# Query halves turned by DMA in an attention and FFN kernel: raw fp16 halves, inverse norms multiplied into the scores

## What is computed

```python
q = (x @ Wq.T).reshape(b, s, H, HD).transpose(0, 2, 1, 3)
k = (x @ Wk.T).reshape(b, s, HKV, HD).transpose(0, 2, 1, 3)
q = _rmsnorm(q, q_norm_w)      # tf * rsqrt(mean(tf * tf) + EPS) * w
k = _rmsnorm(k, k_norm_w)
qg = q.reshape(b, HKV, G, s, HD)
scores = jnp.einsum('bkgqd,bksd->bkgqs', qg, k) / math.sqrt(HD)
attn = jax.nn.softmax(scores + bias[None], axis=-1)
...
return out @ Wo.T
```

## Time and profile before

| what | value |
|---|---|
| median of 3 runs | 728.1 us (727.3 to 729.38) |
| the profiled execution's own time | 728.39 us |
| its span, first to last instruction | 725.1 us |
| PE busy | 709.9 us, 98% |
| DVE, ACT, POOL busy | 497.4, 453.3, 452.4 us |
| share of the chain that ended last on PE | 86% |
| DMA, share of 16 engines | 21.7% |

### The profile page before, as it was taken

One profiled execution on the slowest core, in us unless ns is written; L12 is line 12 of the kernel. 1 busy time (PEld: TensorE's weight loads), 2 busy tenths in 40 slices (PEclk: granted clock), 3 DMA queues, 4 the chain that ended last, 5 costly groups with the idle time before them and its releaser, 6 DMA issues.

```text
span 725.1 us, 14838 instructions
## 1 busy us (share of the span) xinstructions
PE 709.9 (98%) x5322; PEld 429.3 (59%) x5322; DVE 497.4 (69%) x777; ACT 453.3 (63%) x1325; POOL 452.4 (62%) x380
## 2 busy tenths in 40 slices
PE   9999999999999999999999999999989999999996
PEld 8766565665656566565665656566535555555554
DVE  5978777577666757767675775575665777777776
ACT  0578475764856667484574747547556677767664
POOL 0468774844855675484376648438427778868885
PEclk9999999999999999999999999999999999999999
DMA  7410433242332232234233122221000000010001
GB/s 263 180 61 2 171 107 106 83 133 72 116 131 91 98 124 64 72 116 159 72 116 130 58 78 82 74 74 30 2 1 1 0 1 0 1 44 17 0 1 58
DMA packets 21737, 54.18 MB, mean 75 GB/s; under 512 B 3744, under 2 KB 4288, under 8 KB 19520
## 3 DMA queue, kind: packets, MB, share of 16 engines
q1 hardware_dynamic: 21552, 53.41, 21.7%
q10 hardware_dynamic: 144, 0.26, 0.1%
HBM read 51.57 MB, written 2.10 MB: 74 GB/s over the span
## 4 chain that ended last, share of the span: by engine, by line
PE 86%; POOL 5%; DVE 4%; DMA 2%; issue 1%; SPq 1%; ACT 1%; DVEq 0%; POOLq 0%
PE bank L561 20%; PE bank L563 20%; PE bank L562 20%; PE bank L698 3%; PE bank L901 3%; PE bank L902 3%; PE bank L876 3%; PE bank L877 3%; PE bank L740 2%; POOL wqlo L1883 1%; DMA xT<-in_xt 1%; PE bank L888 1%; PE bank L705 1%; PE bank L889 1%; PE bank L725 1%
## 5 line engine op out<-in xcount | busy, mean ns | idle before, releaser
L561 PE MATMUL bank<-wohi,oThi 128*128 128x512 f16 x256 | 97.1, 379 | 2.1 <-DVE oTlo L1577 2.1
L561 PE MATMUL bank<-wqhi,cThi 128*128 128x512 f16 x256 | 97.0, 379 | 1.4 <-POOL wqlo L1883 0.6
L563 PE MATMUL bank<-wohi,oTlo 128*128 128x512 f16 x256 | 97.0, 379 | 0.0
L562 PE MATMUL bank<-wolo,oThi 128*128 128x512 f16 x256 | 97.0, 379 | 0.0
L563 PE MATMUL bank<-wqhi,cTlo 128*128 128x512 f16 x256 | 97.0, 379 | 0.0
L562 PE MATMUL bank<-wqlo,cThi 128*128 128x512 f16 x256 | 97.0, 379 | 0.0
L1900 POOL TENSOR_TENSOR qinv<-qms,neghalf 128x8 f32<-128x8 f32 x32 | 52.7, 1646 | 46.5 <-ACT qms L1074 46.5
L1893 POOL TENSOR_TENSOR wolo<-wor,wohi 128x512 f16<-128x512 f32 x32 | 36.4, 1157 | 70.8 <-ACT wohi L1037 70.8
L1066 ACT ACTIVATE qsq<-qraw 128x128 f32<-128x128 f32 x256 | 75.8, 299 | 4.7
L1585 DVE SCALAR_TENSOR_TENSOR x<-bank,ysc,x 128x512 f32<-128x512 f32 x64 | 48.0, 750 | 44.2 <-PE bank L563 43.7
L1907 POOL TENSOR_TENSOR qn<-qraw,qinv 128x512 f32<-128x512 f32 x64 | 68.6, 1092 | 4.2 <-POOL qinv L1900 3.2
(11 more groups left out here) (209 smaller groups left out, 1886.0 us busy)
## 6 DMA issues: line engine op xcount, KB each, us to landing
wqr<-in_wq SPq DMA_DIRECT2D x8, 1024.0 KB, 4.8
wor<-in_wo SPq DMA_DIRECT2D x8, 1024.0 KB, 4.8
raw<-in_gu_w SPq DMA_DIRECT2D x28, 256.0 KB, 2.9
zeros<-in_gu_z SPq DMA_DIRECT2D x28, 256.0 KB, 3.6
wkvr<-in_wkv SPq DMA_DIRECT2D x8, 512.0 KB, 4.2
srow<-in_up_s SPq DMA_DIRECT2D x14, 256.0 KB, 4.2
raw<-in_dn_w SPq DMA_DIRECT2D x14, 256.0 KB, 3.2
zeros<-in_dn_z SPq DMA_DIRECT2D x14, 256.0 KB, 4.5
```

The source lines that it names most:

```text
L561: mm(o, ahi, bhi, start=start and k == 0, stop=False)
L562: mm(o, ahi, blo, start=False, stop=False)
L563: last = mm(o, alo, bhi, start=False, stop=stop and k == n - 1)
```

## The change

The inverse norm no longer touches the queries. POOL scales the raw query tile by a power of two and rounds it to fp16 (`query_high`, the new high half), DVE computes the low half from the same raw tile (`queries_low`), and both go side by side into `qpair`, rows on partitions. Four DMA transposes for two tiles, eight a unit, turn `qpair` into `qT`, each for one batch slot of 32 rows: 32 partitions x 16 blocks x 128 values of 2 bytes, 128 KB (`turn_queries`). Sixteen small DMAs a unit (32 partitions x 4 floats) carry the inverse norms from the row layout of the queries to the row layout of the scores (`move_norms`). DVE multiplies them by the constant factor (`qsc`), multiplies the scores by `qsc`, and then adds the bias in an instruction of its own. `transpose_q` and `queries_high` are gone.

```
+TURNED = 16 * 2 * BQ
+MOVED = 16 * BQ
...
-        qn = sb("qn", [P, HQ, G, HD], F32, att)
+        qpair = sb("qpair", [P, HQ, 2, G, HD], F16, att)
...
-        qhi = sb("qhi", [P, HB, G, S], F16, att)
-        qlo = sb("qlo", [P, HB, G, S], F16, att)
+        qT = sb("qT", [P, 2, BQ, 2, 2, G, S], F16, att)
...
+            def turn_queries(u, j):
+                if u and j == 0:
+                    sp.wait_ge(t_s, u)
+                sp.wait_ge(d_qlo, HQ * u + 2 * j + 2)
+                for b in range(BQ):
+                    sp.dma_start(qT[:, j, b, :, :, :, :].rearrange("p t k g s -> p (t k g) s"),
+                                 qpair[S * b:S * b + S, 2 * j:2 * j + 2, :, :, :].rearrange("p t k g d -> p (t k g) d"),
+                                 transpose=True).then_inc(l_qT, 16)
+
+            def move_norms(u):
+                sp.wait_ge(p_qpow, 2 * u + 2)
+                if u:
+                    sp.wait_ge(d_qsc, u)
+                for b in range(BQ):
+                    for g in range(G):
+                        sp.dma_start(qmoved[S * g:S * g + S, b, :], qinv[S * b:S * b + S, g, :]).then_inc(l_qsc, 16)
...
                 load_up(first)
                 load_down(first)
+                turn_queries(2 * kv, 0)
+                turn_queries(2 * kv, 1)
+                move_norms(2 * kv)
                 load_gate(second)
                 load_up(second)
                 if kv + 1 < HKV:
                     load_wo(kv + 1)
                 load_down(second)
+                turn_queries(2 * kv + 1, 0)
+                turn_queries(2 * kv + 1, 1)
+                move_norms(2 * kv + 1)
...
             def scores(u):
                 pe.wait_ge(d_klo, u + 1)
-                pe.wait_ge(d_qlo, HQ * u + HQ)
+                pe.wait_ge(l_qT, TURNED * u + TURNED)
+                if not (isinstance(u, int) and u == 0):
+                    pe.wait_ge(d_sc, u)
...
-                    if not (isinstance(u, int) and u == 1 and t == 0):
-                        for tq in queries_after(t):
-                            transpose_q(u, tq)
...
             def queries_low(u, t):
-                dve.wait_ge(a_qhi, HQ * u + t + 1)
-                V.tensor_tensor(qlo[:, BQ * t:BQ * t + BQ, :, :].rearrange("p b g s -> p g b s"),
-                                query_bank(u, t)[:, :].rearrange("p (g b s) -> p g b s", g=G, b=BQ),
-                                qhi[:, BQ * t:BQ * t + BQ, :, :].rearrange("p b g s -> p g b s"),
-                                ALU.subtract).then_inc(d_qlo, 1)
+                dve.wait_ge(p_qhi, HQ * u + t + 1)
+                V.scalar_tensor_tensor(qpair[:, t, 1, :, :], qraw[:, t, :, :], V_DOWN, qpair[:, t, 0, :, :],
+                                       ALU.mult, ALU.subtract).then_inc(d_qlo, 1)
 
             def scores_biased(u, kv):
                 first = isinstance(u, int) and u == 0
+                dve.wait_ge(l_qsc, MOVED * G * u + MOVED * G)
+                V.tensor_scalar(qsc[:, :, :], qmoved[:, :, :].rearrange("p b t -> p t b"), scale[:, 0:1], None,
+                                ALU.mult).then_inc(d_qsc, 1)
                 dve.wait_ge(t_s, u + 1)
...
-                V.scalar_tensor_tensor(sc[:, :, :], PB[1][:, :].rearrange("p (b k) -> p b k", k=S), scale[:, 0:1],
-                                       bias[:, None, :].broadcast_to([P, HB, S]), ALU.mult,
-                                       ALU.add).then_inc(d_sc, 1)
+                V.tensor_tensor(sc[:, :, :], PB[1][:, :].rearrange("p (b k) -> p b k", k=S),
+                                qsc[:, :, :].rearrange("p t b -> p (t b)")[:, :, None].broadcast_to([P, HB, S]),
+                                ALU.mult).then_inc(d_scaled, 1)
+                dve.wait_ge(d_scaled, u + 1)
+                V.tensor_tensor(sc[:, :, :], sc[:, :, :], bias[:, None, :].broadcast_to([P, HB, S]),
+                                ALU.add).then_inc(d_sc, 1)
...
+            def query_high(u, t):
+
+                pool.wait_ge(a_qraw, HQ * u + t + 1)
+                if isinstance(u, int) and u == 0:
+                    pool.wait_ge(d_down, 1)
+                elif t == 0:
+                    pool.wait_ge(l_qT, TURNED * u)
+                Q.tensor_tensor(qpair[:, t, 0, :, :], qraw[:, t, :, :],
+                                down[:, :, None].broadcast_to([P, G, HD]), ALU.mult).then_inc(p_qhi, 1)
```

More of the change, by code:

```diff
@@ L313, in build @@
         t_kT = sem("t_kT")
[L314 removed]
+        l_qT = sem("l_qT")
+        l_qsc = sem("l_qsc")
         t_s = sem("t_s")
@@ L1073, in query_squares @@
                         act.wait_ge(p_qpow, 2 * u - 1 + t // 2)
-                    A(qms[:, pair, :], qss[:, pair, :], ACT.Identity, bias=eps[:, 0, half:half + 1],
+                    A(qms[:, :, pair], qss[:, :, pair], ACT.Identity, bias=eps[:, 0, half:half + 1],
                       scale=1.0 / HD).then_inc(a_qms, 1)
@@ L1185, in step @@
                 keys_high(u)
-                queries_high(u, 2)
                 if half and last:
                     mix_input(1)
-                queries_high(u, 3)
-                if half and last:
                     mix_input(2)
@@ L1611, in finish @@
                         up_low(2 * kv - 1)
-                    if t == 1 and not half:
+                    if t == 2 and not half:
                         up_low(2 * kv - 2)
@@ L1641, in step @@
                 elif not last:
                     link(weight_max(M_Q, wqr, l_wq, kv + 1))
[L1643 to L1644 removed]
+                queries_low(u, 1)
                 probs_low(u - 1)
+                if half and not last:
+                    scale_wq()
+                if not (half or last):
+                    link(weight_max(M_KV, wkvr, l_wkv, kv + 1))
+                queries_low(u, 2)
                 if u == 2:
                     gate_ints(0)
[L1648 to L1653 removed]
@@ L1654, in step @@
-                outputs_low(u - 1)
-                values_low(u, half)
-                if not half:
-                    down_ints(2 * kv - 2)
+                outputs_low(u - 1)
+                queries_low(u, 3)
+                up_ints(2 * kv - 1 if half else 2 * kv - 2)
+                values_low(u, half, (0,))
+                if half and not last:
+                    scale_wkv()
+                values_low(u, half, (1,))
+                if not half:
+                    weight_max(M_O, wor, l_wo, kv).then_inc(d_mx, 1)
@@ L1658, in step @@
+                down_ints(2 * kv - 1 if half else 2 * kv - 2)
                 if half and not last:
```

209 lines of the change are left out of this document (85 added, 124 removed).

## The result

The changed kernel takes 786.9 us (786.56 to 788.88, 4 runs) against 728.4 us for the kernel before (727.3 to 729.38). The ratio is 1.081, 95% interval 1.079 to 1.083: 8% slower, 58.5 us, where 22.4 us less was forecast. It lies beyond the range (699 to 754).

The account below looks back on a forecast made before the run. PE was taken as the bound, busy 709.9 of 725.1 us. Removed transposes 24.5, less 0.7 for the second score pass and 1.4 for small stalls, gave 22.4 us off the median 728.1: 705.7 us, range 699 to 754.

Parts of the forecast that it names:

- What PE loses: PE, units 2 to 15: 16 query transposes a unit removed, 109 ns each in the stream, 24.5 us gained.
- What SP must do in time: SP's queue each unit: four turns, 16 small issues and landing leave the norms 0.65 us late, inside slack; 1.4 us allowed.
- rival 3: SP becomes the bound through 24 issues a unit, from T = 1.76; about 753 us at T = 2.2; chance 0.20.
- T: Time for which one DMA transpose holds SP, taken as 1.2 us; first stall at 1.24.
- rival 2: Norms partly replace the transposes' cost: T 1.24 to 1.76 or small DMAs a microsecond later; 714 us to no change; chance 0.15.
- the ceiling: Upper limit for T, from SP's longest issues in the trace, 1.55 and 1.89 us, where its queue was called full.
- break-even at T = 1.76: On SP, the T at which a pair of steps loses the 3.5 us it gains, by 8T - 10.6.
- What the other engines gain or lose: ACT, POOL and DVE: POOL's multiply and DVE's low half at nothing; second score pass costs 0.7 us once, behind the last unit.
- Units 0 and 1 at nothing: At the start: 3.5 us of removed transposes counted at nothing, since about 3 us are lost to later norms.
- Halves landing in time: Turned query halves: last turn issued by 322.8, scores start about 330.4, so 7 us to land.
- `load_gate` adds no term: SP's load behind the 24 issues lands near 335; its reader becomes late only at T near 1.5, so no cost.
- The Trainium skill's two figures: DMA transposes of a unit's 1 MB: 261 GB/s, estimated 4 us, against 1309 ns per 128x128, estimated 42 us.

Follow-up runs that it names:

- the run with six fewer: Kernel before with 6 of the 16 query transposes of each unit from 2 on left out, nothing else changed: 718.8 us, ratio 0.989.
- the complete kernel at the end: Against the changed kernel: norms multiplied into queries, DMA transposes kept, single score pass, keys earlier on POOL, DVE pieces moved; nothing left out: 717.5 us, ratio 0.985.
- the ceiling as forecast: Changed kernel without the small DMAs and with DMA transposes for units 0 and 1 alone: 727.8 us, where 704.6 was expected.
- the keys ahead: Changed kernel without the small DMAs, with second power, key power and keys ahead of the expert-weight scaling on POOL: 718.4 us, ratio 0.988.
- the kernel with half of the norms: Changed kernel with 8 small DMAs a unit instead of 16, half of the norms not moved: 730.7 us, ratio 1.002 to 1.006.
- run with VectorE copies: Changed kernel, complete, with the norms moved by 16 small VectorE copies a unit instead of 16 DMAs and a scaling pass: 793.8 us.

## Why the prediction was wrong

**What PE loses: right.** 101 ns a transpose by the steps of the run with six fewer and 114 by its medians, 109 in the sum; and the complete kernel at the end comes within 0.4 us a pair of the steps that the term promised.

**What SP must do in time: the step that failed, by the sizes of its terms.** The sum had the norms land 0.65 us late, inside the slack; in the steady part DVE waited 48.9 us for them, and the step came to 33.85 us. The mechanism was named, and it was rival 3's, with chance 0.20, though its condition (T from 1.76) was not met. The terms of the round, measured from one turning of probabilities to the next:

| term | forecast | measured |
|---|---|---|
| probabilities turned, to the last low half | 7.6 (318 - 310.37) | 8.6 |
| four turns | 4.8 | 5.2 |
| sixteen small issues | 7.6 | 10.1 |
| landing | 1.8 | 1.15 |
| landed norms to turned probabilities | 6.2 or 6.9 | 7.7 |
| round | 28.0 or 28.7 | 32.7 |

The forecast columns are the prediction's own numbers, the last from the rows of its two kinds of step (5.5 + 0.7 and 6.5 + 0.4). Against PE's own steps of 28.9 and 29.4 us they leave 0.9 and 0.7 us (the prediction, which took the times of one step for both kinds, left itself 0.85 and 0.15), and every term but one came out over. The largest part, 2.5 of the 4.0 to 4.7 us by which the round is longer, is the small DMAs: 0.63 us each with their gaps, where I took a price from plain loads (0.46 to 0.52) and allowed for a microsecond more in rival 2 alone. T, on which I hung the whole decision, was nearly right: a median of 1.28 us against 1.2. That was in part luck: no view shows that SP's queue was full at the two longest issues, as I wrote of the ceiling, and at the one of 1.89 us the DMA engines were 31% busy, as in the steady part. So "break-even at T = 1.76" was a threshold in the wrong variable. In the last term I had forgotten `qsc` itself (0.37 us to the first pass) and what the new lists put into the chain. In a step with `half` a high half of the next queries stands on POOL between the subtraction and `pr`:

```profile
344.00 1.05 POOL L1908 TENSOR_TENSOR sc<-sc,smax 128x512 f32<-128x512 f32 x1 [3.46 <-DVE smax L1546]
345.01 1.04 POOL L1886 TENSOR_TENSOR qpair<-qraw,down 128x512 f16<-128x512 f32 x1
346.00 1.60 POOL L1877 TENSOR_TENSOR wolo<-wor,wohi 128x512 f16<-128x512 f32 x1
347.57 1.49 POOL L1915 TENSOR_TENSOR pr<-ex,srec 128x512 f32<-128x512 f32 x1
```

DVE's sum is done only 0.1 us ahead of that (347.48), since `gint` waited there too, 1.1 us for its load. In a step without `half`, POOL waits for DVE, and DVE for the load of `gint`, which went out behind the norms:

```profile
313.32 0.69 DVE L1578 TENSOR_TENSOR gint<-raw,zeros 128x512 f16<-128x512 int32 x1 [2.05 <-DMA zeros<-in_gu_z]
```

In the steps with `half` the turns start late too: SP's list holds them behind the load of the output weights. SP's timeline of the next step:

```profile
351.20 0.33 SPq L505 DMA_DIRECT2D wor<-in_wo  x1
```

All eight then follow from 352.58 and end at 363.74, the small DMAs end at 373.88, the norms are there at 375.02, and PE turns the next probabilities at 382.58: a step of 33.5 us. What eight turns in a row cost is little, since the last four would wait for their low halves anyway (358.54 and 5.2 us give 363.7).

The groups of issues, with min/median/max of one in ns, then of the landing in us:

```profile
L531 SPq DMA_TRANSPOSE qT<-qpair x128: 1202/1282/1992, 43.0 to 566.4; - x128
...
DMA to landing us min/median/max: 2.7/2.8/6.5
```

```profile
L541 SPq DMA_DIRECT2D qmoved<-qinv x256: 507/591/1366, 54.5 to 577.7; - x128
...
DMA to landing us min/median/max: 1.6/1.7/4.6
```

**What the other engines gain or lose: wrong, a miss that no rival held.** "Both at nothing" was said of POOL's multiply and DVE's low half. The low half grew from 685 to 904 ns in the mean (996 without the norms' stall). The larger mistake was to take over the time of the keys: "the keys are done at about 323.7", 13.3 us behind the turned probabilities and "hidden by 1 us", rested on POOL's `raw` waiting for nothing, as at 319.62 before. With the DMAs out of the steady steps the keys were done 15.7 us behind, because POOL waits for DVE's `raw`, which the new list takes 7.8 us later. The sum put that order at nothing, and it is worth 9 of the 23 us between the ceiling as forecast (704.6) and as measured (727.8). Of the rest, 4.4 us lie before unit 2 and some 6 us in the steady part (steps of 29.58 us where 29.1 was forecast), of which PE's waits for `pr` are 3.9. The second pass over the scores (0.69 us) is one part of that chain; it was never taken out by itself, so that it costs nothing isn't shown.

**Units 0 and 1 at nothing: wrong.** The first norm was issued at 54.5 us and DVE had them at 65.7, where the prediction had 50.5 and 61 at the latest. The changed kernel loses 21.5 us before unit 2. Without the small DMAs it is 9.1, so 12.4 are theirs, the same serial queue; 4.4 are left even with the keys ahead, and unit 0's turns are 0.9 of the first 5.0. (The range's lower end, 699, doesn't follow from the terms either: 705.7 - 3.5 - 1.4 is 700.8.)

**Halves landing in time: right.** PE waited for `qT` once, in the start of the last kernel. **`load_gate` adds no term: wrong in part.** `gint` waited 20.1 us for it in 13 steps, and in the steps without `half` it is what makes the last term longer. It isn't a cause by itself: the kernel with half of the norms is rid of the loss with the loads still behind eight turns. **The Trainium skill's two figures**: eight turns, 1 MB, are issued in 10.8 to 11.2 us and landed 2.8 us behind the start of the last one, 12.3 us in all (in the last kernel from 82.34 to 94.68, where PE waited for them). That is neither the 42 us estimated from VectorE: DVE Perf Modes (The three transpose paths) nor the 4 us estimated from DMA: Bandwidth & Descriptors (Latency and other measured facts); the issue on SP sets it here.

## What to carry to other kernels

When an edit puts work on a queue that feeds a later step of the same chain, sum one round of the loop term by term and set it against the step of the engine that bounds: a round of five estimates that comes out 1 us under isn't hidden. Here a DMA's price was first the time that its issuing engine was held: sixteen of 512 bytes held SP for 10.0 us, about as long as eight transposes of 128 KB (10.9), while the DMA engines were 4% busy. When the list of an engine is rewritten around an edit, follow each wait to what is now queued behind it: one line moved on POOL was worth 9 us. With the norms back in the queries and a few more pieces moved, the same DMA transposes ran 1.5% faster than the kernel before.

## What the runs showed of the hardware

- A DMA transpose from SBUF to SBUF of 32 partitions x 2048 fp16 values holds SP for 1.28 us in the median (changed kernel) and lands 2.8 us after its issue starts.
- A DMA of 512 bytes holds SP for 0.59 us and ACT for 0.61 us in the median; in the same trace plain loads of 256 KB to 1 MB held SP for 0.33 to 0.43 us in the median.
- A VectorE instruction on 32x4 numbers takes 223 ns in the median (208 at least, run with VectorE copies).
- A TensorE transpose of 128x128 float32 values in a stream was worth 101 to 114 ns (run with six fewer).
- After a stall of 2.7 us PE ran at the lower clock for some 3 us; where something else set the step, having the clock back gave some 4 of 787 us.
- A DVE instruction with both operands in SBUF took 996 ns in the mean beside POOL's work and 768 with 64 of POOL's instructions gone.
